# Attention and mixture-of-experts kernel: padding writes split into pairs, small steps of each body moved, 28 idle products and four more early tiles

## What is computed

```python
def layer(x, ctx):                       # x 16 x 256 x 256, ctx 16 x 77 x 192
    x = x + xattn(layernorm(x), ctx)     # 16 heads of 64; the last 4 context rows are a second set of keys
    x = x + ffn(layernorm(x))
def xattn(t, ctx):
    q = t @ Wq + lora(t)                 # rank 32, the same for k, v and the output
    k, v = ctx[:73] @ Wk + lora, ctx[:73] @ Wv + lora
    o = softmax(q k / 8) v + softmax(q kipa / 8) vipa      # per head
    return o @ Wo + bo + lora(o)
def ffn(t):                              # 8 experts, width 512, 2 per token
    top, idx = top_k(t @ gate_w, 2)
    w = softmax(top)
    return sum over the two picks of w * (silu(t @ w1[e]) @ w2[e])
```

## Time and profile before

| | |
|---|---|
| median of 3 runs | 741.42 us (741.09 to 745.17) |
| the profiled execution | 745.7 us, of which 743.7 us is the span of the profile |
| TensorE busy | 674.2 us, 91% of the span |
| VectorE, GpSimd, ScalarE busy | 548.5, 495.5, 455.4 us |
| weights, splits and first products | 0 to about 76 us |
| bodies 0 to 14 | about 76 to 466 us, one body of the loop 26.5 us |
| body 15 and the passage | about 466 to 502 us |
| FFN, 39 tiles | about 502 to 744 us, 5.7 us for a tile in its steady part |

### The profile page before, as it was taken

One profiled execution on the slowest core, in us unless ns is written; L12 is line 12 of the kernel. 1 busy time (PEld: TensorE's weight loads), 2 busy tenths in 40 slices (PEclk: granted clock), 3 DMA queues, 4 the chain that ended last, 5 costly groups with the idle time before them and its releaser, 6 DMA issues.

```text
span 743.7 us, 22841 instructions
## 1 busy us (share of the span) xinstructions
PE 674.2 (91%) x7980; PEld 560.0 (75%) x7981; DVE 548.5 (74%) x1239; ACT 455.4 (61%) x768; POOL 495.5 (67%) x582
## 2 busy tenths in 40 slices
PE   6637799999999999999999999779979999999994
PEld 2226688788778878878877887568869888888993
DVE  3953778898898898889889889875737555555552
ACT  1435878778777877877877787544624344434441
POOL 3115546877887887788778788765666656665665
PEclk9997999999999999999999999899989999999998
DMA  9911101211211112121121121133655654454550
GB/s 268 321 48 47 31 21 34 75 33 46 76 38 52 62 45 62 46 74 33 46 76 43 47 63 48 42 99 77 147 132 103 96 91 85 80 90 80 94 79 1
DMA packets 51558, 56.35 MB, mean 76 GB/s; under 512 B 15104, under 2 KB 45824, under 8 KB 51520
## 3 DMA queue, kind: packets, MB, share of 16 engines
q1 hardware_dynamic: 37136, 38.50, 18.1%
q0 software_dynamic: 14384, 17.33, 13.4%
HBM read 30.67 MB, written 25.76 MB: 76 GB/s over the span
## 4 chain that ended last, share of the span: by engine, by line
PE 52%; DVE 17%; issue 10%; SPq 6%; DMA 5%; ACT 5%; POOL 4%; POOLq 1%; DVEq 0%
PE ps L1532 37%; PE ps L1650 5%; DVE pt_s L1268 4%; PE ps L1630 4%; DVE sm L1338 3%; DVE q_s L1268 2%; PE ps L1705 2%; PE ps L529 2%; DVE v_s L1268 2%; POOL out_x L499 2%; DMA out_x<-pt_s,token_of 2%; ACT q_s L1062 1%; DVE x_sb L1363 1%; PE ps L1563 1%; DMA pt_s<-in_wo 1%
## 5 line engine op out<-in xcount | busy, mean ns | idle before, releaser
L499 POOL DMA_INDIRECT out_x<-pt_s,token_of x78 | 124.9, 1601 | 28.4 <-issue 27.2
L588 ACT ACTIVATE q_s<-ps 128x512 f32<-128x512 f32 x78 | 46.5, 596 | 126.9 <-PE ps L1532 123.1
L715 DVE TENSOR_TENSOR wq_s<-q_s,wq_s 128x512 f16<-128x512 f32 x78 | 55.8, 718 | 80.5 <-ACT wq_s L592 65.7
L1532 PE MATMUL ps<-q_s,ffnw 128*128 128x256 f16 x936 | 110.7, 276 | 1.1 <-DVE q_s L697 1.1
L1532 PE MATMUL ps<-ffnw,wq_s 128*128 x936 | 109.1, 273 | 0.1
L894 POOL TENSOR_TENSOR prob<-prob,mx 128x1168 f32<-128x1168 f32 x64 | 77.6, 1234 | 37.8 <-DVE mx L1331 37.8
L1532 PEld LDWEIGHTS ps<-ffnw,wq_s 128*128 128x128 f16 x936 | 89.8, 98 | 14.2 <-issue 2.6
L1532 PEld LDWEIGHTS ps<-q_s,ffnw 128*128 x936 | 91.0, 99 | 12.4 <-issue 1.5
L1532 PE MATMUL ps<-xt_s,wq_s 128*128 128x256 f16 x768 | 90.2, 279 | 1.9 <-DVE xt_s L1268 1.9
L1532 PE MATMUL ps<-wo_s,ot_s 128*128 128x256 f16 x768 | 89.4, 273 | 1.4 <-DVE ot_s L1268 1.4
L1532 PEld LDWEIGHTS ps<-xt_s,wq_s 128*128 128x128 f16 x768 | 76.8, 100 | 13.0 <-issue 1.9
(11 more groups left out here) (210 smaller groups left out, 1230.5 us busy)
## 6 DMA issues: line engine op xcount, KB each, us to landing
prob<-rows_dram SPq DMA_DIRECT2D x39, 264.0 KB
wstage<-in_ffn_w SPq DMA_DIRECT2D x16, 512.0 KB, 3.6
x_sb<-in_x SPq DMA_DIRECT2D x4, 1024.0 KB, 10.7
out_x<-x_sb SPq DMA_DIRECT2D x16, 256.0 KB
rows_dram<-wstage SPq DMA_DIRECT2D x8, 264.0 KB
out_x<-pt_s,token_of POOLq DMA_INDIRECT x78
pt_s<-in_wq SPq DMA_DIRECT2D x2, 512.0 KB, 4.6
pt_s<-in_wo SPq DMA_DIRECT2D x2, 512.0 KB, 8.3
```

The lines of the kernel that those rows point to most:

```text
L499: pool.indirect_dma_start(out_rows, bass.IndirectOffsetOnAxis(ap=token_of[:, j % UNROLL, c:c + 1], axis=0), y_sb[:, j % UNROLL, c, :], Non ...
L588: act.activation(h32[:, half, :], h_ps(t, j, half), ACT.Silu, scale=1 / WSCALE).then_inc(silu_done, 1)
L715: dve.tensor_tensor(hs[:, j % 2, 1, 2 * half:2 * half + 2, :].rearrange("p f n -> p (f n)"), h32[:, half, :], hs[:, j % 2, 0, 2 * half:2 * ...
L1532: last = pe.matmul(o, lhs(a, n), rhs(c, n), start=(i == 0), stop=(i == len(steps) - 1))
```

## The change

`fill_up` writes the blocks of two experts after each of tiles 3, 7, 11 and 15 in place of all eight after tile 3. `EARLY` is 20, so the late tiles begin after tile 15. The late table is computed in two parts, after tiles 7 and 11. In the bodies 1 to 14 `rstd_2` moves ahead of `normalise(b, 1)` on GpSimd, `normalise_2` and `x2t_copy` move forward on ScalarE, and `transpose_2` and `router` on TensorE, with other PSUM banks for keys and heads. In body 15 and behind it TensorE gets 12, 10 and 6 products whose result nobody reads.

```diff
-EARLY = 16
+EARLY = 20
...
-            return ps[:, (5, 1)[k] if isinstance(b, int) and b == 0 else (0, 3)[k], :]
+            return ps[:, (5, 1)[k] if isinstance(b, int) and b == 0 else k, :]
...
-            return ps[:, 4 + k, :]
+            return ps[:, (4, 6, 5, 7)[k], :]
...
             def fill_up(t):
-                if t != UNROLL - 1:
+                if t < UNROLL - 1 or t >= 5 * UNROLL - 1:
                     return
-                sp.wait_ge(pad_made, 5)
-                sp.wait_ge(tab_done, 2)
-                for e in range(EXPERTS):
+                if t == UNROLL - 1:
+                    sp.wait_ge(pad_made, 5)
+                    sp.wait_ge(tab_done, 2)
+                pair = (t - UNROLL + 1) // UNROLL * 2
+                for e in (pair, pair + 1):
...
                 link(dve.tensor_reduce(all_row_of[:, 0:LATE], past_n_late, AX, ALU.add))
+
+            def late_rest():
+                flags = (past_late, past_n_late)
...
# GpSimd, body
                 normalise(b, 0)
                 if routed and not last:
                     scatter(b - 2, 0)
+                if not first and not last:
+                    rstd_2(b - 1)
                 normalise(b, 1)
-                if not first:
+                if last:
                     rstd_2(b - 1)
...
# ScalarE, body
                 pt(b, 1)
+                if not first and not last:
+                    normalise_2(b - 1)
                 pt(b, 2)
...
                 pt(b, 4)
+                if last:
+                    normalise_2(b - 1)
                 pt(b, 5)
-                if not first:
-                    normalise_2(b - 1)
+                if not first and not last:
+                    x2t_copy(b - 1)
                 pt(b, 6)
                 pt(b, 7)
                 ot(b, 0)
-                if not first and not last:
-                    x2t_copy(b - 1)
...
# VectorE, between the tiles
                 if t == 7:
                     late_table()
+                if t == 11:
+                    late_rest()
...
# TensorE
+            def keep_warm(bank, count):
+                for i in range(count):
+                    pe.matmul(ps[:, bank, :], wq_s[:, 0, 0, 0:P], wq_s[:, 0, 1, 0:512], start=True, stop=True)
...
                 new_values(b)
+                if last:
+                    keep_warm(0, 12)
...
                     pe.wait_ge(q_split, 4 * b + 8)
-                    if not first:
-                        pe.wait_ge(slots, b)
+                    pe.wait_ge(v_split, 2 * b + 1)
                     new_keys(b + 1)
...
                 transpose_probs(b, 5)
+                if not first and not last:
+                    pe.wait_ge(pt_split, 8 * b + 2)
+                    transpose_2(b - 1)
                 pe.wait_ge(pt_split, 8 * b + 3)
                 transpose_probs(b, 6)
...
                     if k == 1 and not first and not last:
-                        transpose_2(b - 1)
-                    if k == 2 and not first and not last:
-                        pe.wait_ge(k_split, 2 * b + 4)
+                        pe.wait_ge(slots, b)
                         router(b - 1)
                     attend(b, k)
...
             transpose_2(BATCH - 2)
+            keep_warm(0, 10)
             project(BATCH - 1, 0)
             pe.wait_ge(slots, BATCH - 1)
             router(BATCH - 2)
             project(BATCH - 1, 1)
+            keep_warm(0, 6)
```

More of the change, by code:

```diff
@@ L686, in late_table @@
                 adds(adds_all[:, EARLY:NT], EARLY, LATE, all_starts[:, 0:LATE]).then_inc(tab_done, 1)
-            return full_tiles, early_table, all_rows, late_table
+            return full_tiles, early_table, all_rows, late_table, late_rest
         def ffn_dve(dve, then, late_table):
@@ L964, in body @@
                     scatter(b - 2, 0)
+                if not first and not last:
+                    rstd_2(b - 1)
                 normalise(b, 1)
-                if not first:
+                if last:
                     rstd_2(b - 1)
-                if last:
                     scatter(b - 2, 0)
@@ L1427, in place_rows @@
                 assert c.n == ROUTE, c.n
-            full_tiles, early_table, all_rows, late_table = tile_tables(dve)
+            full_tiles, early_table, all_rows, late_table, late_rest = tile_tables(dve)
             def body(b, first, last):
```

## The result

The changed kernel takes **736.41 us** (median of 9 runs, 734.58 to 739.03) against 744.67 us for the kernel before in the same comparison (741.09 to 747.26): a ratio of 0.9902 [0.9880, 0.9925]. The forecast of 730.7 us had the sign right, and the time lies in its range, but near the upper end, and rival A's 734.9 us is nearer to it. By the two medians 8.3 us came off, by the ratio 7.3 us, where 10.7 us were forecast. Of the 5.7 us between the forecast and the result, 3.3 us are the base: 741.42 us was the median of 3 runs, 744.67 us is that of 9.

The account below looks back on a forecast made before the run. TensorE, busy nearly throughout, was taken as the bound, with small stalls in the bodies and a 4.03 us gap at tile 8. 6.5 + 4.2 + 0 = 10.7 us off 741.42 gave 730.7 us, range 724.0 to 738.0.

Parts of the forecast that it names:

- rival A: Loop bodies gain nothing because ScalarE's queue has no gap left, only the FFN gains; 734.9 us, chance 0.19.
- The padding in pairs: FFN, tile 8: load no longer queued behind eight writes; 3.9 us of stall and 2.6 us of low clock, 6.5 us.
- issued at 538.13: FFN, SyncE: when tile 8's load would go out, landing at 541.22, where TensorE wants it at 541.2.
- The bodies: Loop bodies: moved steps shorten each of 13 bodies by 0.32 us, 4.2 us; bounds 1.3 and 11.7 us.
- from `shift` to `shift` the round is then 26.2 us and no longer 26.5: Loop bodies, GpSimd: its round sets the period, giving 0.32 us in each body.
- the lower bound of 1.3: Loop bodies: if group 3's head outputs hold the next projection, 0.1 us a body, 1.3 us in all.
- a new stall of about 1.1 us: Loop bodies, TensorE: group 4's transposes start at 379.34 instead of 378.16, as GpSimd's second normalisation ends later.
- B: Loop bodies: later normalising moves the whole round, up to 0.95 us lost in each; slower, 747.3 us, chance 0.05.
- D: Loop bodies: all 0.9 us gained in each, as GpSimd's 0.3 us head start adds up; 723.2 us, chance 0.08.
- 0 us: Body 15 and passage to the FFN: idle products gain nothing, GpSimd's last scatter sets the start; bounds 0.5 us either way.
- With the clock kept up to 2.7 us of TensorE time is saved: Body 15: the 32 transposes, 6.35 us before, would take 3.6 us as in the loop.
- The longer `EARLY`, the split table and the bank numbers get nothing: FFN tiles: these edits were put at nothing, since TensorE does not wait for VectorE there.

Follow-up runs that it names:

- the idle products alone: The kernel before with only the 28 idle products added; 744.19 us, 1.0005 of the kernel before.
- the bodies alone: The kernel before with only the moved steps of the loop bodies and their PSUM banks; 742.55 us, 1.0001 of the kernel before.
- the repeat of the change: The changed kernel, nothing altered, measured and profiled again; 735.77 us, 0.9897 of the kernel before.
- the repeat of before: The kernel before, nothing altered, measured and profiled again; 743.26 us, 0.9982.

## Why the prediction was right or wrong

**"The padding in pairs", 6.5 us: right in mechanism, and in size for the profile it was made from.** The load "issued at 538.13" comes out at 533.01; the FFN starts 4.6 us earlier in this profile, so 533.5 was forecast. Bringing the eight writes back costs 6.45 us between medians. At the place itself it is less: the two tiles around the stall take 11.9 to 12.0 us undisturbed, 18.5 in the profile of before (10.69 and 7.85), 17.2 in its repeat (10.56 and 6.62) and 17.3 with the eight writes in the changed kernel (10.16 and 7.10), so 5.2 to 6.5 us. Two more kernels with the eight writes widen that: 16.9 with the idle products alone, 18.7 with the bodies alone. The stall is alike in all (3.7 to 4.3 us); the clock's part varies, with 24 products in 3.70 to 5.29 us where the full clock takes 2.78. The forecast used one draw, 4.95 us, near the slow end. Undisturbed, the two tiles still take 0.6 us more than two others (5.69 each). The rest of the 6.5 us from the first scores lies at the FFN's start, where the last scatter's DMA took 4.53 us there and 3.49 in the repeat of the change. The pairs are 1.55 us long, not 2.7: the second write follows after about 1.25 us and the queue is then free. They cost nothing that shows at the loads behind them, as said, but the 3.09 us for the load was one draw too: it took up to 4.61 us, and then 1.29 us of the stall are there in spite of the pairs.

**"The bodies", 0.32 us each, 4.2 us: the sum against the wrong row.** The body came out at 26.20 us, where 26.2 was forecast. What failed is the step "from `shift` to `shift` the round is then 26.2 us and no longer 26.5". The 26.52 us of the earlier trace rows are one of two periods of the unchanged loop, and the other, 26.29, stands in three of the four profiles. Against it the gain is 0.09 us in a body, 1.2 us, near the lower bound of 1.3 that I had for another reason. Where the extra 0.23 us sits can be read: it is the router's wait for x2t, there in the earlier trace rows and absent in the repeat. Why an execution falls into one or the other was not tried. The stall that the change makes was forecast as "a new stall of about 1.1 us" ahead of group 4; it measured 0.51 there and 0.29 ahead of the keys, 0.80 in all. The second comes from the wait for `v_split` that the change puts before `new_keys`, which I had not costed. Rival A's reason (ScalarE's queue) shows nowhere in TensorE's waits, yet its outcome for the bodies is nearly what was measured. B and D are out: the period is neither above 26.5 nor below 26.2. The rule taken from the Trainium skill (SBUF — State Buffer, on the shared port pair) agrees with the changed kernel's trace: `picked` still takes 1.83 us beside `shift` in the body (0.18 in the FFN), and the bodies alone gave nothing near 9 us. No run tests the rule by itself.

**"0 us" for body 15 and the idle products: without them the changed kernel is 3 to 4 us slower.** Two steps of the reasoning failed. "With the clock kept up to 2.7 us of TensorE time is saved" took the 32 transposes as one run of 3.6 us. They are two of sixteen, and the second starts 3.3 us behind the first, when GpSimd's probabilities are there. With the clock kept they take 5.24 us, so 1.1 us can be saved and not 2.7. And the clock was kept in only two of the eight profiles with the 12 products (the idle products alone, and the kernel without the last 16), with 2.23 and 1.98 us of waiting against 1.97 in the changed kernel. In the changed kernel the stage of the transposes has a granted clock of 0.61:

```profile
475.30:478.40 3.10, 3.05 (x16) 2.67 (x16) 3.06 (x8) 1.79 (x4) 2.37 (x2) 0.61 0.00 0
```

What decides between the two was not found. And the ten and six products "lie ahead of tile 0's load" and were taken as costing and giving nothing, because the profile of before shows the FFN's start at full clock. There the last scatter took 2.44 us. In the repeat it took 2.43, but in the eleven others whose chain of waits shows it 2.93 to 4.59, and without idle products the wait is then long enough to lose the clock: 4.39 to 5.74 us from the first tile's products to the second's in all four kernels without the last 16 whose scatter took 3.68 us or more, against 3.27 or 3.28 in all eight with them, with scatters up to 4.53 us. Both profiles of the kernel before have the short scatter and no other has, so whether the changes themselves lengthen it is open. The Trainium skill (DMA: Bandwidth & Descriptors, Latency and other measured facts) gives the memory's access as 0.2 us on average and 2 us at high load; the spread seen here is of that size, but no run here shows that load is its cause. Alone, on the unchanged bodies, the idle products gave nothing measurable, and this agrees with the forecast; on the changed kernel the last 16 give about 2 us (1.9 between medians; 4.0 in the profiles, less the 1.7 at tile 8), the first 12 nothing (0.7 us between medians, 0.0 in the profiles).

**"The longer `EARLY`, the split table and the bank numbers get nothing": off by about 0.9 us the other way.** From the products that follow tile 8's to GpSimd's last scatter-add it takes 184.1 us before (554.10 to 738.17) and 185.0 us after (542.98 to 727.98). The four profiles with 16 early tiles and the old padding have 184.0 to 184.7 us. The nine with 20 have 184.9 to 185.5, but for one of 186.5 (the change without idle products). The padding pairs in this stretch are not the reason, since the kernel with all eight blocks at once has 185.4. In the changed kernel TensorE has two waits there that neither profile of before has, and that come again in the repeat of the change:

```profile
618.14 2.79 PE L1542 MATMUL ps<-q_s,ffnw 128*128 128x256 f16 x24 [0.24 <-issue]
621.25 2.81 PE L1542 MATMUL ps<-ffnw,wq_s 128*128 x24 [0.32 <-issue]
```

Going back to 16 tiles did not bring the time back, and that kernel has 187.6 us there, with waits of its own such as the one shown. The cause stays open.

**The account.** From the first scores, the repeat of before has 670.8 us and the change 666.1, 4.7 us less. Tile 8 and the one behind it give 17.2 - 12.0 = 5.2 us, and the stretch up to the last scatter 420.9 - 418.9 = 2.0 (the 13 bodies 1.2 of it). The way from that scatter to the first tile's products takes 1.4 us more (9.6 to 11.0), and 1.0 us is given back in the later tiles: 4.8. These two executions took 743.34 and 735.31 us, 8.0 apart: 3.1 of that lie ahead of the first scores (70.48 against 67.37), where nothing was forecast. No experiment ties this start to the change.

The profiles from which the forecast was made and checked give another sum. From the first scores the profile of before has 676.5 us, the change 10.3 less. The two tiles give 18.5 - 12.0 = 6.5 us, the stretch up to the last scatter 5.2 (13 bodies of 0.32 us are 4.2), the passage takes 0.5 more (10.5 to 11.0) and the later tiles 0.9 more. So between these two executions the two terms of 6.5 and 4.2 us came out, and what was put at nothing nearly cancels. The step that failed is to take the difference off the median: the profiled execution of before was 4.3 us above the median, with the long period and a slow draw of the clock behind the stall, and part of what the change removed there the other executions did not have. That the time still fell into the range, although the bodies gave 1.2 us against the usual period, is in part luck, because the start's 3.1 us fill the gap between those two executions.

All but one of the executions of before lay between 739.1 and 750.2 us over all comparisons. How often each period and each start occurs was not counted.

## What to carry to other kernels

When a queue's writes hold back a load that TensorE needs, what counts is the writes ahead of that load, not their number: spread them so that each group fits into the queue's idle time. Before you cost an edit from a loop's period, profile the unchanged kernel twice; the 0.23 us by which the two periods differ were most of the 0.32 us that I forecast. And do not take a gain that was read from one slow execution off the median. Idle products paid here only where they lasted until the awaited data arrived, and their worth doesn't show in a profile in which the wait happened to be short.

## What was not expected of the hardware

- One loop, two steady periods: 26.52 us with a 0.23 us wait of the router in each body, and 26.29 us without, in different executions of the same program.
- The same indirect DMA of the last scatter takes from 2.43 to 4.59 us until its completion is seen; the repeat of the changed kernel took 3.49 us where its first profile had 2.93.
- The load of tile 8 took from 3.09 us to 4.61 us (the change without the last 16 idle products).
- The start of the first scores, behind the loading of the weights, lay between 66.46 and 71.03 us.
- Twelve products at the full clock, then 2 us of waiting at a granted clock of 1.00, had two outcomes: 0.61 in the transposes that followed in the changed kernel (1.97 us of waiting), 1.00 in the kernel without the last 16 products (1.98 us) and in the idle products alone (2.23 us).
- SyncE's padding writes leave about 1.33 us apart in a row of eight (9.61 us for all, less 0.3 for the last, over seven), 1.25 us in a pair.
